# Edge stage of a graph-network kernel: windows of 16 destinations with a PSUM bank each, instead of 32 destinations over two banks

## The reference, cut to what matters

```python
src = jax.random.randint(..., (80000,), 0, 2500)
dst = (2500 * jax.random.uniform(..., (80000,)) ** 2.0).astype(int)
order = argsort(dst); src = src[order]; dst = dst[order]        # edges sorted by destination
def _sage(x, src, dst, W_l, b_l, W_r):
    msg_sum = segment_sum(x[src], dst, num_segments=2500)       # sum over the edges of a destination
    cnt = segment_sum(ones, dst, num_segments=2500)
    return (msg_sum / maximum(cnt, 1)[:, None]) @ W_l.T + b_l + x @ W_r.T
```

## Time and profile before

| | us |
|---|---|
| median of 3 runs (1825.84 to 1829.18) | 1827.98 |
| the profiled execution | 1833.38 |
| its span | 1831.6 |
| first register load to last key of the edge stage | 47.9 to 434.5 |
| DVE busy over the whole span | 966.3 |
| PE busy over the whole span | 1674.0 |

### The profile page before, as it was taken

How to read it: one execution, slowest core, us unless ns; L and a number is a source line. 1 busy time by engine, 2 the same in 40 slices (tenths; PEclk the granted TensorE clock), 3 DMA queues, 4 the chain that set the end, 5 groups by cost and what they waited for, 6 DMA issues and landing times. The chain is left out here.

```text
span 1831.6 us, 31389 instructions
## 1 busy us (share of the span) xinstructions
PE 1674.0 (91%) x9423; PEld 1104.4 (60%) x9424; DVE 966.3 (53%) x2821; ACT 669.4 (37%) x1352; POOL 235.8 (13%) x290
## 2 busy tenths in 40 slices
PE   6889888987979899999799899999997989998998
PEld 5344555665747423333656799999955557644657
DVE  7888889887568664244511100000055874345862
ACT  3112444674024576665121344444321432201220
POOL 2100000001010003900044000000065000500002
PEclk8999999999989999999599999999998999999989
DMA  2000121225750000000513312211121002141001
GB/s 85 0 15 29 59 87 67 107 116 194 236 155 7 1 1 1 1 1 1 188 58 115 132 66 90 84 63 66 63 84 34 1 1 82 58 145 42 1 1 60
DMA packets 86409, 118.86 MB, mean 65 GB/s; under 512 B 6789, under 2 KB 72511, under 8 KB 86177
## 3 DMA queue, kind: packets, MB, share of 16 engines
q1 hardware_dynamic: 80992, 106.53, 17.2%
q0 software_dynamic: 3936, 10.37, 1.8%
q10 hardware_dynamic: 1376, 0.66, 0.1%
HBM read 70.66 MB, written 46.87 MB: 64 GB/s over the span
## 5 line engine op out<-in xcount | busy, mean ns | idle before, releaser
L804 PE MATMUL bank<-onehot_key,onehot_low 128*128 128x320 bf16 x1304 | 223.4, 303 | 38.2 <-DVE onehot_low L603 23.8
L599 DVE TENSOR_SCALAR onehot_key<-iota_keys,edge_keys 128x640 bf16<-128x640 f16 x652 | 231.5, 381 | 27.5 <-PE bank L804 22.7
L804 PEld LDWEIGHTS bank<-onehot_key,onehot_low 128*128 128x128 bf16 x1304 | 104.3, 99 | 147.9 <-DVE onehot_key L599 55.0
L2647 ACT ACTIVATE hidden<-bank,b_cols 128x128 f32<-128x128 f32 x344 | 126.4, 367 | 178.2 <-PE bank L2574 154.7
L2728 DVE TENSOR_TENSOR slot_columns<-bank,b_rows 128x256 f32 x43 | 18.3, 425 | 290.3 <-PE bank L2580 290.3
L2574 PEld LDWEIGHTS bank<-slot_columns,w 128*128 128x128 f32 x1376 | 162.8, 194 | 5.6 <-issue 3.4
L2574 PE MATMUL bank<-slot_columns,w 128*128 x1376 | 163.2, 278 | 3.2 <-issue 3.2
L2580 PE MATMUL bank<-w,hidden 128*128 128x256 f32 x688 | 155.6, 379 | 0.0
L671 ACT ACTIVATE edge_low_shifted<-edge_low,window_offset 128x631 f32 x81 | 66.7, 823 | 192.1 <-DVE onehot_low L603 191.2
L2580 PEld LDWEIGHTS bank<-w,hidden 128*128 128x128 f32 x688 | 127.4, 190 | 15.5
L1739 ACT ACTIVATE XT<-bank 128x512 f32<-128x512 f32 x160 | 84.3, 603 | 57.8 <-PE bank L1667 57.8
(11 more groups left out here) (517 smaller groups left out, 2745.4 us busy)
## 6 DMA issues: line engine op xcount, KB each, us to landing
AT_dram<-at_strip SPq DMA_DIRECT2D x20, 640.0 KB, 4.0
A_dram<-a_strips SPq DMA_DIRECT2D x20, 640.0 KB, 2.9
sg_strip<-AT_dram SPq DMA_DIRECT2D x20, 640.0 KB, 4.0
back_strip<-A_dram SPq DMA_DIRECT2D x24, 480.0 KB, 5.0
w<-in_L_ffn_W1p SPq DMA_DIRECT2D x8, 1024.0 KB, 5.3
w<-in_L_ffn_W2p SPq DMA_DIRECT2D x8, 1024.0 KB, 7.8
slot_rows<-ty_zero SPq DMA_DIRECT2D x1, 6144.0 KB, 24.5
slot_columns<-slot_rows SPq DMA_DIRECT2D x12, 512.0 KB, 8.7
```

The lines of the kernel that those rows point to most:

```text
L599: dve.tensor_scalar(ohk[:, q, :], ioh[:, :], key[:, ds(chunk(n, offset, q), 1)], None, ALU.is_equal).then_inc(s_key[q], 1)
L804: last = pe.matmul(bank[2 * (x % 2) + h][:, 0:HB], ohl[q // 2][:, :, q % 2], ohk[:, q, h * HB:(h + 1) * HB], start=False, stop=q == Q - 1, ...
L2647: act.activation(hid[:, f, 0:P], bank[f % 4][:, 0:P], ACT.Gelu, bias=b1[:, ds((e + 1) * FB + f, 1)]).then_inc(s_rg, 1)
```

## The change

The window is 16 destinations (`HD`), so there are 160 windows; a key is 320 wide, and each window has one bank and one matmul per chunk. Two windows of the same 32 destinations (h = 0, 1) share the shift, the copy and the transposes, which stay as they were ("block"). Groups have two chunks (Q = 2) with two key buffers and one pair of lows, which is now written between the two keys of a group. The rounding to even addresses goes; the offset is unpacked with more register arithmetic. Register loads still fetch four windows at a time, now of 16 destinations. The tables from which the ranges come have 160 columns instead of 80.

```diff
-            FQ, Q, SHIFT = 2, 4, 16
-            BIAS = (1 << SHIFT) - 2 * Q * GRP
+            FQ, Q, SHIFT = 2, 2, 10
             WD = 32
-            KW, HB, NW, XW, SB = WD * T, WD * T // 2, NP // WD, P // WD, T // (P // WD)
+            HD = WD // 2
+            KW, HB, NW, XW, SB = WD * T, HD * T, NP // HD, P // WD, T // (P // WD)
+            BLOCKS, HW, FETCH = NP // WD, NP // HD // 2, 4
...
-                ohk = sb(tmp, "onehot_key", [P, Q, KW], bf16)
-                ohl = [sb(tmp, f"onehot_low{h}", [P, P, 2], bf16) for h in range(Q // 2)]
+                ohk = sb(tmp, "onehot_key", [P, Q, HB], bf16)
+                ohl = sb(tmp, "onehot_low", [P, P, Q], bf16)
...
-                    offset = eng.compute_val(packed & (2 ** SHIFT - 1))
+                    offset = eng.compute_val((packed & (2 ** SHIFT - 1)) + BIAS - before * Q)
...                                                                       # DVE
-                            even = dve.compute_val(offset + (offset & 1))
+                            keys = ioh[:, h * HB:(h + 1) * HB]
                             def group(n):
                                 for q in range(Q):
+                                    if q == Q - 1:
+                                        dve.wait_ge(s_used[q], n + 1)
+                                        dve.tensor_tensor(ohl[:, :, :], iow[:, :, :], spread(shifted[x % 2][:, ds(chunk(n, offset, 0), Q)], 1, P), ALU.is_equal).then_inc(s_low, 1)
                                     dve.wait_ge(s_used[q], n + 1)
-                                    dve.tensor_scalar(ohk[:, q, :], ioh[:, :], key[:, ds(chunk(n, offset, q), 1)], ...).then_inc(s_key[q], 1)
-                                    if q % 2 == 0:
-                                        h = q // 2
-                                        dve.wait_ge(s_used[q + 1], n + 1)
-                                        dve.tensor_tensor(ohl[h][:, :, :], iow[:, :, :], ...).then_inc(s_low[h], 1)
+                                    dve.tensor_scalar(ohk[:, q, :], keys, key[:, ds(chunk(n, offset, q), 1)], ...).then_inc(s_key[q], 1)
-                            dve.wait_ge(s_shift, w + 1)
+                            if h == 0:
+                                dve.wait_ge(s_shift, w // 2 + 1)
                             dve.wait_ge(s_fused, w + 1)
...                                                                       # PE
                             def group(n):
+                                pe.wait_ge(s_low, n + 2)
                                 for q in range(Q):
                                     pe.wait_ge(s_key[q], n + 1)
-                                    if q % 2 == 0:
-                                        pe.wait_ge(s_low[q // 2], n + 1 + q // 2)
-                                    for h in range(2):
-                                        last = pe.matmul(bank[2 * (x % 2) + h][:, 0:HB], ohl[q // 2][:, :, q % 2], ohk[:, q, h * HB:(h + 1) * HB], ...)
-                                    last.then_inc(s_used[q], 1)
+                                    pe.matmul(into, ohl[:, :, q], ohk[:, q, :], ...).then_inc(s_used[q], 1)
...
                             with pe.Fori(before, following[0]) as n:
                                 group(n)
+                            if h == 0:
+                                return following
                             if t >= 1:
                                 turn(t - 1, 1 - k, x)
                                 forward(t - 1, 1 - k, x)
```

More of the change, by code:

```diff
@@ L300, in graph_stage @@
             most = NW * (CH // Q + 1)
-            assert most < 2 ** (31 - SHIFT) and Q * most < BIAS and CH + FQ < 2 * Q * GRP
+            BIAS = 1 << (Q * most).bit_length()
+            assert most < 2 ** (31 - SHIFT) and CH < 1 << SHIFT and NW % FETCH == 0 and HW <= P
             tmp = ExitStack()
@@ L378, in chunk @@
                 def chunk(n, offset, q):
[L380 to L385, removed]
+                    return nc.s_assert_within(n * Q + offset + (FQ + q - BIAS), 0, CHP - 1, skip_runtime_bounds_check_because=
                                               "a window ends at most FQ + Q chunks past its first, or Q - 1 past its last")
@@ L610, in window @@
                             for q in range(FQ):
-                                dve.tensor_scalar(fok[:, q, :], ioh[:, :], key[:, ds(chunk(before, offset, q - FQ), 1)], None, ALU.is_equal).then_inc(s_fkey[q], 1)
+                                dve.tensor_scalar(fok[:, q, :], keys, key[:, ds(chunk(before, offset, q - FQ), 1)], None, ALU.is_equal).then_inc(s_fkey[q], 1)
                             following = parts(dve, packed)
@@ L676, in window @@
                             following = load_next()
-                            act.wait_ge(s_low[1], before + 1)
-                            shift(w + 1, (x + 1) % 2, following)
+                            act.wait_ge(s_low, before + 1)
+                            shift(w + 1, (x + 1) % 2)
                             begun = not isinstance(i, int) or i > 0
@@ L712, in forward_copy @@
                             act.activation(AG[:, ds(t, 1), :].rearrange("p t c -> p (t c)"), bank[6 + k][:, 0:FW], ACT.Copy).then_inc(s_fc, 1)
-                        shift(0, 0, load(act, 0))
+                        shift(0, 0)
                         halves(2 * early + 1)
                         turned(early + 2)
-                        windows(act, window, AHEAD)
+                        blocks_of_windows(act, window, AHEAD)
                         total = load(act, NW)[0]
@@ L812, in window @@
+                            pe.wait_ge(s_flow, 2 * block + h + 1)
                             for q in range(FQ):
-                                pe.wait_ge(s_fkey[q], w + 1)
-                                for h in range(2):
-                                    last = pe.matmul(bank[2 * (x % 2) + h][:, 0:HB], fol[:, :, q], fok[:, q, h * HB:(h + 1) * HB],
-                                                     start=q == 0, stop=False, skip_group_check=True)
+                                pe.wait_ge(s_fkey[q], 2 * block + h + 1)
+                                last = pe.matmul(into, fol[:, :, q], fok[:, q, :], start=q == 0, stop=False, skip_group_check=True)
```

101 lines of the change are left out of this document (49 added, 52 removed).

## The result

The changed kernel takes 2007.96 us (median of 4 runs, 2006.71 to 2008.75) against 1827.37 for the kernel before beside it: ratio 1.0987, 95% interval 1.0968 to 1.1006. The forecast was 1970 with a range of 1900 to 2030: the sign and the mechanism hold, the size is 38 us short. All times here are medians of undisturbed runs; one of ten runs of the kernel before at odd addresses took 4246.71 us and is left out of its median.

What follows compares the result with a forecast made beforehand. DVE sets the edge stage's pace, its sequencer only 0.1 us behind being the bound. Windows 301, repetitions 143, loads 40 and 5, products 15, clock 20 make 524 against 386.6 us; with 3.5 ahead, 1970 us, range 1900 to 2030.

Steps and rivals of the forecast that it cites:

- ring of a repetition: Edge-stage loops: low to PE's matmul, its release to DVE's next key, key to low; 1.18 us each, 143 us.
- odd addresses: Without rounding, about half the windows read lows at odd 2-byte addresses; taken as nothing, upper bound 8 us.
- low clock: PE at 1.2 GHz in the long loops, lengthening the hand-over of about 100 repetitions by 0.175 us; 20 us in all.
- late first chunks: A few of the windows' first chunks delayed on PE by the low clock, counted within its 20 us.
- TensorE's products: Root matmuls and x products on PE hold DVE up through first chunks or key buffers; 15 us, bounds 5 and 30.
- its loads meeting a repetition: Where a register load meets a loop repetition, PE's own load delays the matmul too; 5 us.
- windows and register loads: DVE's sequencer bounds 160 windows at 1.88 us, 301 us; 40 register loads of 0.96 us, nothing hidden, 40 us.
- Rival 1: Edge stage: the sequencer alone sets the pace, a repetition costs 0.91 us; total 1906 us, chance 0.13.
- Rival 2: Edge stage: DVE's engine stays the bound and narrow keys pay; faster, total 1769 us, chance 0.05.
- rival 3: PE at 1.2 GHz through the whole stage, first chunks late in every block; total 2049 us, chance 0.08.
- The check of the sum before: Old kernel's edge stage: DVE's work 322 us plus waits gives 368 of 386.6, leaving 19 us for small gaps.
- Ahead of the stage: Table operations and a reduction before the edge stage double their length; 3.5 us more.

Runs made afterwards that it cites:

- even starts: Kernel after with every window's start rounded down to an even chunk, so all lows lie at even addresses: 1996.18 us, ratio 1.0904.
- constant matmuls: Kernel after with five matmuls of a constant (128 x 128) ahead of each group's wait on TensorE: 1975.09 us, ratio 1.0789.

## Why the prediction was right, and where it was short

The terms of the stage's sum, forecast and measured:

| term | forecast | measured |
|---|---|---|
| ring of a repetition, full clock, even address | 121 x 1.18 = 143 | 121 x 1.192 = 144 |
| odd addresses | 0 | 11 (even starts) |
| low clock, late first chunks with it | 20 | 31 (constant matmuls) |
| TensorE's products (15) and its loads meeting a repetition (5) | 20 | about 35 (constant matmuls): 18 products, 9 loads, 8 other |
| windows and register loads | 301 + 40 = 341 | 337, by difference |
| stage | 524 | 558 |

- *The ring.* Right in size and in all three parts; the kernel with groups of four supports that it is the ring, since with two more buffers, and a third of the repetitions, 106 of 118.7 us of the wait went. Rival 1, the sequencer alone, is out: no low in window 0 comes under 1.19 us after the last. Rival 2, VectorE's engine as the bound, is out too: it is busy 345 us of the 563 from 48 to 611.
- *Odd addresses: the step that was wrong and not only short.* "I take nothing" was wrong. A low of 256 elements takes 0.41 to 0.42 us at an odd address and 0.28 at an even one, the 4-byte pace that I had as the upper bound of the earlier trace rows. The Trainium skill had both views; "VectorE: DVE Perf Modes" (Mode 2x_1P), which asks for 4-byte alignment, agrees with these 0.41 and 0.28 us, and section 5.1 of "Vector Engine (DVE) Microarchitecture Reference", by which alignment made no difference, does not. I should have taken 8, and counted the first lows too.
- *The clock: under-sized.* I counted the dearer hand-over (0.14 us a repetition, near my 0.175) but only "a few late first chunks". The low clock went on past the long loops (0.68 to 0.87 from 200 to 611 us), so PE was late behind its sums also in short windows. Of the 31 us that the constant matmuls won in the stage 21 lie in the repetitions and 10 in the windows. Of rival 3 this is a small part: not every block, and at 0.95 us only where it falls.
- *Products and loads: under-sized.* In the kernel with constant matmuls, where a repetition is 1.192 or 1.325 us by its start's parity, the 121 intervals from low to low sum to 186.7 against 151.8 for the ring alone (64 and 57 of them). 31 of these 35 us lie in 23 intervals over 1.8 us, up to 5.8. Sorted by what TensorE did in them, nine intervals with products hold 18 us (forecast 15), ten that meet its register load hold 9 (forecast 5), and the other 102 hold 8, for which the forecast had no term. In the kernel after, at its low clock, the nine with products hold 30 over the same ring. So the products were about right at the full clock, and what was short is the loads, the rest, and the clock under the products. The trace sorts these parts; no run isolates them.
- *Windows: over-sized.* 1.77 us, not 1.88, mostly since the new address operations cost 0.13 and not 0.22 (1.64 us with the offset out of the table). 160 x 1.77 = 283, with 32.6 behind loads 316; some 21 of the 337 have no name.
- *The check of the sum before.* It counts the 6.7 us wait for ACT in the stage, but the stage is measured from the end of that wait (47.9). So the check leaves 26 us of the 386.6 without a name, not 19. The forecast does not use this number, but such a remainder was there before the change as well.
- *Loads.* 40 x 0.97 as forecast, of which 32.6 us show as idle time.
- *Ahead of the stage.* 4.9 us, not 3.5; but other variants of this kernel start the stage at 49.1 to 53.1, so single executions don't tell.

Too little by 1, 11, 11 and 15 us and too much by 4 make the 34 us; since the windows' 337 us are what the other terms leave of 558, this sum closes by construction. The three terms that were short had bounds of 0 to 8, 0 to rival 3 and 5 to 30, and each was taken in the lower half of its bounds.

## What to carry to other kernels

Before loop bodies are made smaller, count the buffers that let the producer run ahead: with as many buffers as a body fills, each repetition pays the whole ring of both engines (here 1.19 to 1.47 us for two chunks, against 0.63 to 0.84 with four buffers). A consumer that idles in such a ring can also lose its clock (a mean of 0.58 here), which makes the ring longer (1.33 us for 1.19); so price both together. Halving the width of the windows here doubled their number and left VectorE with no fewer instructions in the stage (1323, before 1218), and the shorter one (0.21 for 0.30 us) didn't pay that back.

## What the runs showed of the hardware that I had not expected

- A register load's time grows with its entries: 0.30, 0.52, 0.97 us for 1, 2, 4, and mostly 5.7 us for 16 on VectorE (3.8 on TensorE). Fewer and longer loads cost 18 and 37 us; shorter ones won 7 to 12.
- A 256-element comparison of 2-byte numbers takes 0.41 to 0.42 us at an odd element and 0.28 at an even one.
- 1405 added matmuls in the idle time of TensorE made the kernel 33 us faster, by a granted clock of 0.88 to 0.99 in place of 0.58 to 0.87.
